# Projection and routing stage: the weights of the chosen experts made on GpSimd instead of VectorE

## The chip, the cores and the metric

One core of one Trainium2 chip runs the whole kernel. The metric is the device time of one execution in microseconds. Times of the trace are counted from the start of the profiled execution's span.

## The reference, cut to what matters

The model has two layers, each with an attention and a mixture of experts. Only the stage behind the first attention is touched: projection, layer norm, residual, layer norm, and the choice of 6 of 64 experts for each of N = 8192 tokens.

```python
x = x + _layernorm(attention(x) @ w_proj)
logits = _layernorm(x) @ router_weight.T
scores = jax.nn.sigmoid(logits)
_, top_idx = jax.lax.top_k(scores + expert_bias[None, :], K)        # E = 64, K = 6
top_scores = jnp.take_along_axis(scores, top_idx, axis=1)
probs = top_scores / (jnp.sum(top_scores, axis=-1, keepdims=True) + 1e-20)
```

## The kernel before

The kernel is a chain of phases with a barrier of all engines between them. The phase in question, `phase_project_route` (tiles prj_...), works on 16 blocks of 512 tokens. A block is four tiles of 128 tokens (TPB = 4), with the tokens on the partitions; j is the block's parity and picks one of two buffers. The program of each engine is written by hand, in order, with semaphores. `pipeline(e, stages, 4)` runs the steps: in step n each engine calls `stages(a, b, c, d)` with a = block n, b = block n-1, c = block n-2 and d = block n-3, so that four blocks are in work at a time. There are 19 steps; a block that isn't there yet or any more is None.

- a: VectorE divides the attention output by its denominators (L988, `att`), ScalarE rounds it to `ah` (L1089), VectorE makes the rest `al` (L1048).
- b: TensorE multiplies by the projection, 24 matmuls into `y_ps`. VectorE takes mean and variance (L745 to L750), GpSimd makes 1/sqrt as a power of -0.5 (L949), VectorE the shift (L756), ScalarE the normalised `yn` (L1095, four instructions), GpSimd the residual sum `xo` (L954).
- c: VectorE takes the statistics of `xo`, GpSimd the power (L945), VectorE the shift (L756), ScalarE writes the normalised rows to `xn[:, j, t, 0:C]` (L1083, four instructions). TensorE turns them, ScalarE and VectorE make the two parts `xh` (L1103) and `xl` (L1052).
- d: TensorE makes the logits (24 matmuls), ScalarE the sigmoid `sc` (L1072). VectorE chooses: `choose` adds the bias, finds the largest with MAX8, copies 6 of them to `pick` beside two fill values (L1009), replaces them (L1012) and writes the 0/1 `mask` (L1014). TensorE packs the mask (L1155). VectorE's `weigh` multiplies the scores by the mask, sums over the experts, adds 1e-20, takes the reciprocal and writes the 64 weights to `xn[:, j, :, C:XW]`, beside the rows of the same tokens (L1023 to L1028). SyncE (SP) stores `xn[:, j]`, rows and weights together, to `expert_rows` (L905).

`xn` has two buffers. ScalarE waits ahead of L1083 until the stores out of `xn[:, j]` that belong to the block two before have landed:

```python
e.wait_ge(r_stored[j], R_STORES)
e.wait_ge(x_scale, 1)
```

SP's queue holds, in each step: load of x, store of xo; stores of xh and xl; loads of the attention output and denominators; store of the packed mask; store of xn. `step` (class Chain) makes an engine wait for its own last instruction before it goes on.

Of the kernel before, what the change touches and what calls it, by code (L numbers as in the profile page):

```python
# [8 lines left out]
ALU = mybir.AluOpType  # L9
ACT = mybir.ActivationFunctionType  # L10
AX = mybir.AxisListType


B, T, C = 8, 1024, 256
N = B * T
NH, HD = 16, 16
P = 128
# [20 lines left out]
def take(eng, *pairs):  # L38

    for sem, n in pairs:  # L40
        eng.sem_inc(sem, -n)  # L41
# [718 lines left out]
def phase_project_route(nc, layer, o_d, rden_d, x_d, wp_d, rw_d, rb_d, yb_d, xo_d, xh_d, xl_d, xg_d, rt_d):  # L760
# [7 lines left out]
    with Phase(nc, f"prj{layer}") as ph:  # L768
# [24 lines left out]
        sb = ph.sb("sb", [P, TPB, E + 8 - K])  # L793
        rep = ph.sb("rep", [P, TPB, E + 8 - K])
        top = ph.sb("top", [P, TPB, 8])
        pick = ph.sb("pick", [P, TPB, 8])
        mask = ph.sb("mask", [P, TPB, E])
        ssum = ph.sb("ssum", [P, TPB])
        rt = ph.sb("rt", [E, 2, BLK // PACK])
# [45 lines left out]
        choice_turned = ph.sem("choice_turned")  # L845
        rt_ready = ph.sem("rt_ready")
        weights_ready = ph.sem("weights_ready")
        xo_seen = ph.sem("xo_seen")
        xo_stored = [ph.sem(f"xo_stored{j}") for j in range(2)]
        x_stored = [ph.sem(f"x_stored{j}") for j in range(2)]  # L850
# [16 lines left out]
        with nc.Block() as block:  # L867
# [61 lines left out]
            @block.gpsimd  # L929
            def _(e):  # L930
                step = Chain(e, pool_chain)
                identity(e, step, ident)
                step(e.memset(digits[:], 0.0))
                for n in range(PACK):
                    step(e.affine_select(out=digits[:], in_=digits[:], compare_op=ALU.not_equal,
                                         fill=float(2 ** (PACK - 1 - n)), base=-n, pattern=[[-PACK, P // PACK]],
                                         channel_multiplier=1))
                step(e.memset(mhalf[:], -0.5))
                e.sem_inc(pe_consts, 1)
                step.close()  # L940

                def stages(a, b, c, d):
                    if c is not None:
                        e.wait_ge(xvar_ready, 1)
                        e.tensor_tensor(rs[:, 1], ve[:, 1], mhalf[:], ALU.pow).then_inc(xrstd_ready, 1)  # L945
                        take(e, (xvar_ready, 1))
                    if b is not None:
                        e.wait_ge(yvar_ready, 1)
                        e.tensor_tensor(rs[:, 0], ve[:, 0], mhalf[:], ALU.pow).then_inc(yrstd_ready, 1)  # L949
                        j = b[1]  # L950
                        e.wait_ge(x_loaded[j], 16)
                        e.wait_ge(xo_stored[j], 16)
                        e.wait_ge(yn_ready, 1)
                        e.tensor_tensor(xo[:, j], x[:, j], yn[:], ALU.add).then_inc(xo_ready, 1)  # L954
                        take(e, (yvar_ready, 1), (x_loaded[j], 16), (xo_stored[j], 16), (yn_ready, 1))

                pipeline(e, stages, 4)

            @block.vector
            def _(e):  # L960
                step = Chain(e, dve_chain)
                e.wait_ge(den_loaded[0], 16)
                e.reciprocal(den[:, 0], den[:, 0]).then_inc(rden_ready[0], 1)
                e.wait_ge(den_loaded[1], 16 * (B - 1))
                e.reciprocal(den[:, 1:B], den[:, 1:B]).then_inc(rden_ready[1], 1)
                e.wait_ge(w_loaded, 48 if layer == 0 else 64)
                split_weights(e, step, wf, wh, wl)
                step(e.memset(sb[:, :, E:E + 8 - K], 3e38))
                step(e.memset(pick[:, :, K:8], 3e38))
                e.sem_inc(pe_consts, 1)  # L970
                step.close()

                def residual(j):
                    e.wait_ge(xo_ready, 1)
                    e.sem_inc(xo_seen, 1)
                    variance(e, step, xo[:, j], st[:, 1], mv[:, 1], ve[:, 1], xvar_ready)
                    take(e, (xo_ready, 1))

                def projected():
                    e.wait_ge(y_ready, 1)  # L980
                    if layer == 1:
                        step(e.tensor_tensor(y[:], y_ps[:], ybias[:].unsqueeze(1).broadcast_to((P, TPB, C)), ALU.add))
                    variance(e, step, y, st[:, 0], mv[:, 0], ve[:, 0], yvar_ready)
                    take(e, (y_ready, 1))

                def divide(j):
                    e.wait_ge(o_loaded[j], 4 * 16)
                    e.tensor_tensor(att[:], o[:, j], rden[:, j], ALU.mult).then_inc(att_ready, 1)  # L988
                    take(e, (o_loaded[j], 4 * 16))

                def softmax_shift():
                    e.wait_ge(logits, 1)
                    step(e.reduce_max(lmax[:], l_ps[:], AX.X))
                    e.tensor_tensor(ls[:], l_ps[:], lmax[:].unsqueeze(2).broadcast_to((P, TPB, E)), ALU.subtract
                                    ).then_inc(shifted, 1)
                    take(e, (logits, 1))

                def choose(j):
                    e.wait_ge(scores, 1)
                    if layer == 1:  # L1000
                        step(e.reduce_sum(ssum[:], sc[:, j], AX.X))
                        step(e.reciprocal(ssum[:], ssum[:]))
                        step(e.tensor_tensor(sc[:, j], sc[:, j], ssum[:].unsqueeze(2).broadcast_to((P, TPB, E)), ALU.mult))
                    step(e.tensor_tensor(sb[:, :, 0:E], sc[:, j], rbias[:].unsqueeze(1).broadcast_to((P, TPB, E)),
                                         ALU.add))
                    for t in range(TPB):
                        e.max(top[:, t], sb[:, t, 0:E])
                    step.settle()
                    step(e.tensor_copy(pick[:, :, 0:K], top[:, :, 0:K]))  # L1009

                    for t in range(TPB):
                        e.match_replace(rep[:, t], pick[:, t], sb[:, t], -3e38)  # L1012
                    step.settle()
                    choice = e.tensor_scalar(mask[:], rep[:, :, 0:E], -1e38, None, ALU.is_lt)  # L1014
                    if layer == 0:
                        choice.then_inc(choice_ready, 1)
                        step.settle()
                    else:
                        step(choice)
                    take(e, (scores, 1))  # L1020

                def weigh(j):
                    step(e.tensor_tensor(sc[:, j], sc[:, j], mask[:], ALU.mult))  # L1023
                    step(e.reduce_sum(ssum[:], sc[:, j], AX.X))
                    step(e.tensor_scalar(ssum[:], ssum[:], 1e-20, None, ALU.add))
                    step(e.reciprocal(ssum[:], ssum[:]))
                    weights = xn[:, j, :, C:XW] if layer == 0 else mask[:]
                    e.tensor_tensor(weights, sc[:, j], ssum[:].unsqueeze(2).broadcast_to((P, TPB, E)), ALU.mult  # L1028
                                    ).then_inc(weights_ready if layer == 0 else choice_ready, 1)

                def stages(a, b, c, d):
                    if c is not None:
                        residual(c[1])
                    if b is not None:
                        projected()
                    if c is not None:
                        scaling(e, mv[:, 1], rs[:, 1], nmr[:, 1], xrstd_ready, x_scale)
                    if a is not None:
                        divide(a[1])
                    if layer == 1 and d is not None:  # L1040
                        softmax_shift()
                    if b is not None:
                        scaling(e, mv[:, 0], rs[:, 0], nmr[:, 0], yrstd_ready, y_scale)
                    if d is not None:
                        choose(d[1])
                    if a is not None:
                        e.wait_ge(ah_ready, 1)
                        e.tensor_tensor(al[:], att[:], ah[:].bitcast(fp32), ALU.subtract).then_inc(al_ready, 1)  # L1048
                        take(e, (ah_ready, 1))
                    if c is not None:  # L1050
                        e.wait_ge(xh_ready, 1)
                        e.tensor_tensor(xl[:, c[1]], t_ps[:], xh[:, c[1]].bitcast(fp32), ALU.subtract  # L1052
                                        ).then_inc(xl_ready, 1)
                        take(e, (xh_ready, 1))
                    if d is not None:
                        weigh(d[1])
                    step.close()

                pipeline(e, stages, 4)
# [1759 lines left out]
```

## Time and profile before

| what | us |
|---|---|
| median of 3 runs | 3260.66 (3260.47 to 3262.6) |
| the profiled execution | 3258.48 |
| its span | 3256.8 |
| VectorE busy over the span | 2225.7 (68%) |
| TensorE matmuls busy | 2842.0 (87%) |
| GpSimd busy | 731.5 (22%) |

The phase lies between about 1080 and 1353 us of the span. Busy shares are sums over the whole kernel; what a change in this phase is worth is read from this phase. A row of the timeline gives start, duration, engine, line, operation, output and inputs, how many instructions it merges, and in brackets the idle time ahead of it with what ended it.

### The profile page before, as it was taken

Reading aid. Unit: us, or ns where it says so; the run is one execution under the profiler, and the core shown is the slowest. Engines: PE = TensorE matmul, PEld = TensorE weight load, DVE = VectorE, ACT = ScalarE, POOL = GpSimd, SP = SyncE. Lnnn points to the kernel's source line nnn. Section 1 sums busy time; section 2 is a strip of 40 time slices with the busy share of each in tenths; the row PEclk is TensorE's granted clock in tenths of the full one; section 3 lists DMA queues with packets and bytes.
Section 4 is the critical chain, followed back from the end, with each engine's and each line's share of the span. In section 5 each row is a group of like instructions: output and inputs, shape, how many; then the busy total and the mean of one; then the engine's idle time right before and its main releaser. Section 6 shows DMA issues by size and latency. Waiting matters only on the chain. (4 is left out here: it accounts for less than half of the span.)

```text
span 3256.8 us, 59136 instructions
## 1 busy us (share of the span) xinstructions
PE 2842.0 (87%) x20033; PEld 2062.9 (63%) x20033; DVE 2225.7 (68%) x6134; ACT 1603.0 (49%) x2446; POOL 731.5 (22%) x882
## 2 busy tenths in 40 slices
PE   7959999999999387689947777998399999999998
PEld 6834444444444276578836664555388888888887
DVE  6768999999997388663338883444466666666664
ACT  3506777777777244333325544544244444444443
POOL 1022222222222133247744422222000000000000
PEclk9959999999999666699968888999699999999999
DMA  6984556666662377648857867653432424243331
GB/s 244 330 153 83 108 115 112 112 112 116 112 110 65 127 270 269 214 138 225 221 165 269 296 228 228 183 162 100 132 99 74 122 65 117 78 102 92 90 86 46
DMA packets 342662, 485.87 MB, mean 149 GB/s; under 512 B 58832, under 2 KB 203248, under 8 KB 342384
## 3 DMA queue, kind: packets, MB, share of 16 engines
q1 hardware_dynamic: 331776, 468.94, 52.1%
q0 software_dynamic: 10240, 14.16, 2.3%
q8 instruction: 85, 1.39, 0.2%
q10 hardware_dynamic: 496, 0.84, 0.1%
q14 instruction: 65, 0.53, 0.1%
HBM read 278.77 MB, written 204.53 MB: 148 GB/s over the span
## 5 line engine op out<-in xcount | busy, mean ns | idle before, releaser
L551 ACT ACTIVATE att_pr<-att_e_ps 128x1024 f32<-128x1024 f32 (+2 forms) x640 | 567.3, 938 | 203.8 <-PE att_e_ps L603 203.8
L579 PE MATMUL att_m_ps<-att_ks,att_qs 63*128 63x512 f32 (+3 forms) x1536 | 465.9, 433 | 40.2 <-PEq L41 31.7
L513 DVE CUSTOM_DVE_ANT_0 att_kept<-att_m_ps,att_causal 128x256 f32<-128x256 f32 (+3 forms) x1024 | 448.5, 488 | 50.3 <-DVEq L41 21.9
L579 PEld LDWEIGHTS att_m_ps<-att_ks,att_qs 63*128 63x128 f32 x1536 | 234.3, 189 | 370.6 <-DVE att_mx L516 148.5
L492 POOL TENSOR_SCALAR_AFFINE_SELECT att_pr<-att_pr 128x256 f32<-128x256 f32 (+1 forms) x384 | 181.4, 485 | 698.0 <-PEq L594 694.5
L516 DVE TENSOR_REDUCE att_mx<-att_m_ps 128x1 f32<-128x512 f32 x512 | 323.3, 684 | 21.5 <-PE att_m_ps L579 17.5
L623 PE MATMUL att_o_ps<-att_pr,att_vs 128*32 128x512 f32 (+3 forms) x3072 | 328.7, 501 | 3.7 <-issue 2.0
L2604 ACT ACTIVATE fin_hh<-fin_hid 128x512 fp32r<-128x512 f32 x192 | 121.4, 632 | 399.8 <-DVE fin_hid L2450 302.2
L603 PE MATMUL att_e_ps<-att_qs,att_ks 64*128 64x512 f32 (+3 forms) x1536 | 269.1, 376 | 6.7 <-ACT att_pr L551 3.3
L2343 POOL TENSOR_TENSOR fin_rs<-fin_ve,fin_mhalf 128x4 f32<-128x4 f32 x48 | 48.4, 1007 | 928.6 <-POOLq L41 928.6
L2446 DVE TENSOR_TENSOR fin_hid<-fin_gate,fin_u_ps 128x512 f32<-128x512 f32 x192 | 131.5, 685 | 136.4 <-ACT fin_gate L2598 82.9
L738 PE MATMUL fin_f_ps<-fin_fhd,fin_hh 128*128 128x256 f32 x768 | 219.5, 286 | 0.2 <-DVE fin_hl L2465 0.2
L738 PE MATMUL fin_f_ps<-fin_fhd,fin_hl 128*128 128x256 f32 x768 | 216.3, 282 | 0.0
L738 PE MATMUL fin_f_ps<-fin_fld,fin_hh 128*128 128x256 f32 x768 | 216.2, 282 | 0.0
L2465 DVE TENSOR_TENSOR fin_hl<-fin_hid,fin_hh 128x512 fp32r<-128x512 f32 x192 | 132.5, 690 | 104.5 <-ACT fin_hh L2604 100.8
L1949 DVE TENSOR_TENSOR lin_am<-lin_a_ps,lin_tri 128x512 f32<-128x512 f32 x128 | 88.5, 692 | 143.5 <-PE lin_a_ps L2032 143.5
L603 PEld LDWEIGHTS att_e_ps<-att_qs,att_ks 64*128 64x128 f32 x1536 | 150.1, 187 | 38.8 <-ACT att_pr L551 13.5
L738 PE MATMUL fin_u_ps<-fin_xh,fin_fhu 128*128 128x512 f32 x384 | 153.0, 398 | 0.0
L738 PE MATMUL fin_g_ps<-fin_xh,fin_fhg 128*128 128x512 f32 x384 | 152.5, 397 | 0.0
L738 PE MATMUL fin_g_ps<-fin_xh,fin_flg 128*128 128x512 f32 x384 | 151.9, 396 | 0.0
L738 PE MATMUL fin_u_ps<-fin_xh,fin_flu 128*128 128x512 f32 x384 | 151.6, 395 | 0.0
L738 PE MATMUL fin_u_ps<-fin_xl,fin_fhu 128*128 128x512 f32 x384 | 151.5, 394 | 0.0
(332 smaller groups left out, 6921.2 us busy)
## 6 DMA issues: line engine op xcount, KB each, us to landing
fin_raw<-weights SPq DMA_DIRECT2D x32, 1024.0 KB, 9.6
att_qs<-q_high SPq DMA_DIRECT2D x128, 128.0 KB, 5.2
att_ks<-k_high SPq DMA_DIRECT2D x128, 128.0 KB, 6.5
attended<-att_ot SPq DMA_DIRECT2D x64, 256.0 KB, 8.5
acc<-att_zero SPq DMA_DIRECT2D x64, 256.0 KB, 2.2
moe_w<-w SPq DMA_DIRECT2D x128, 128.0 KB, 3.4
lqk_a<-acc SPq DMA_DIRECT2D x32, 512.0 KB, 6.0
attended<-lin_ot SPq DMA_DIRECT2D x32, 512.0 KB, 3.7
```

The costliest lines, as they stand in the source:

```text
L492: e.affine_select(out=blk, in_=blk, compare_op=ALU.is_ge, fill=0.0, base=0, pattern=lead + [[1, P]], channel_multiplier=-1).then_inc(maske ...
L513: e.tensor_tensor_reduce(kept[:, n % MBUF, 0:w], m_ps[:, n % MBUF, 0:w], causal[:, BLK - w:], 1.0, -3e38, ALU.add, ALU.max, mx[:, h, at, q ...
L516: e.reduce_max(mx[:, h, at, q:q + 1], m_ps[:, n % MBUF, 0:w], AX.X).then_inc(m_free, 1)
L551: e.activation(out, src, ACT.Exp).then_inc(exp_done, 1)
L579: e.matmul(m_ps[:, (2 * i + n) % MBUF, 0:w], qs[rows, j, p, q * P:(q + 1) * P], ks[rows, j, p, h * BLK:h * BLK + w], start=True, stop=True ...
L603: i = e.matmul(e_ps[:, s % 2, n, m * w:(m + 1) * w], ks[rows, j, p, k * P:(k + 1) * P], qs[rows, j, p, (h + 1) * BLK - w:(h + 1) * BLK], s ...
L623: i = e.matmul(o_ps[32 * hd:32 * hd + 32, BLK - w:BLK], vs[:, j, k, hd * VW:hd * VW + 32], pr[:, u % NPR, hd // 2, hd % 2, 0:w], start=k = ...
L738: i = e.matmul(out, a, b, start=first and n == 0, stop=last and n == len(terms) - 1, **kw)
L1949: e.tensor_tensor(am[:, n % 2, 0:F // 2].rearrange("p (r h) q -> p r h q", h=2), a_ps[:, 0:2, 0:2 * P].rearrange("p r (h q) -> p r h q", h=2),
L2446: product_ = e.tensor_tensor(hid[:, c % 2], gate[:, c % 2], u_ps[:, c % 2], ALU.mult)
L2465: e.tensor_tensor(hl[:, c % 3], hid[:, c % 2], hh[:, c % 3].bitcast(fp32), ALU.subtract).then_inc(hl_ready, 1)
L2604: e.activation(hh[:, c % 3], hid[:, c % 2], ACT.Copy).then_inc(hh_ready, 1)
```

## The change

In `phase_project_route` alone. VectorE's `weigh` goes; GpSimd does the same work for block d behind its residual sum of block b. It multiplies scores by mask, adds the two halves of the 64 values six times (32, 16, 8, 4, 2, 1 values for each token), adds 1e-20, raises to the power -1 and multiplies. Two semaphores are new: VectorE tells GpSimd that the mask is ready (mask_ready), and waits before it writes the next mask until GpSimd has read this one (mask_read). The copy to `pick` goes: MAX8 now reads all 66 columns of `sb`, of which two hold 3e38, so its eight largest are the two fill values and the six chosen, and serve the replacement directly.

```diff
-        pick = ph.sb("pick", [P, TPB, 8])
+        minus1 = ph.sb("minus1", [P, TPB])
+        half = ph.sb("half", [P, TPB, E // 2])
...
+        mask_ready = ph.sem("mask_ready")
+        mask_read = ph.sem("mask_read")
...
+                step(e.memset(minus1[:], -1.0))
...
                         e.tensor_tensor(xo[:, j], x[:, j], yn[:], ALU.add).then_inc(xo_ready, 1)
                         take(e, (yvar_ready, 1), (x_loaded[j], 16), (xo_stored[j], 16), (yn_ready, 1))
+                    if d is not None:
+                        j = d[1]
+                        e.wait_ge(mask_ready, 1)
+                        step(e.tensor_tensor(sc[:, j], sc[:, j], mask[:], ALU.mult))
+                        e.sem_inc(mask_read, 1)
+                        src, n = sc[:, j], E // 2
+                        while n:
+                            step(e.tensor_tensor(half[:, :, 0:n], src[:, :, 0:n], src[:, :, n:2 * n], ALU.add))
+                            src, n = half, n // 2
+                        step(e.tensor_scalar(ssum[:], half[:, :, 0], 1e-20, None, ALU.add))
+                        step(e.tensor_tensor(ssum[:], ssum[:], minus1[:], ALU.pow))
+                        e.tensor_tensor(xn[:, j, :, C:XW], sc[:, j], ssum[:].unsqueeze(2).broadcast_to((P, TPB, E)),
+                                        ALU.mult).then_inc(weights_ready, 1)
+                        take(e, (mask_ready, 1))
+                        step.close()
+
+                e.sem_inc(mask_read, 1)
...
-                step(e.memset(pick[:, :, K:8], 3e38))
...
-                        e.max(top[:, t], sb[:, t, 0:E])
+                        e.max(top[:, t], sb[:, t])
                     step.settle()
-                    step(e.tensor_copy(pick[:, :, 0:K], top[:, :, 0:K]))
                     for t in range(TPB):
-                        e.match_replace(rep[:, t], pick[:, t], sb[:, t], -3e38)
+                        e.match_replace(rep[:, t], top[:, t], sb[:, t], -3e38)
                     step.settle()
-                    choice = e.tensor_scalar(mask[:], rep[:, :, 0:E], -1e38, None, ALU.is_lt)
-                    if layer == 0:
-                        choice.then_inc(choice_ready, 1)
-                        step.settle()
-                    else:
-                        step(choice)
+                    e.wait_ge(mask_read, 1)
+                    e.tensor_scalar(mask[:], rep[:, :, 0:E], -1e38, None, ALU.is_lt).then_inc(choice_ready, 1)
+                    step.settle()
+                    e.sem_inc(mask_ready, 1)
+                    take(e, (mask_read, 1))
                     take(e, (scores, 1))
-
-                def weigh(j):
-                    step(e.tensor_tensor(sc[:, j], sc[:, j], mask[:], ALU.mult))
-                    step(e.reduce_sum(ssum[:], sc[:, j], AX.X))
-                    step(e.tensor_scalar(ssum[:], ssum[:], 1e-20, None, ALU.add))
-                    step(e.reciprocal(ssum[:], ssum[:]))
...
-                    if d is not None:
-                        weigh(d[1])
```

## Rows read from the trace of the kernel before

**Rows 1.** Busy us (instructions) of PE, PEld, DVE, ACT, POOL in one step; clock, DMA.

```profile
1200.89:1214.79 13.90, 11.06 (x66) 9.80 (x66) 11.68 (x43) 6.39 (x13) 4.53 (x3) 0.62 0.83 284
```

**Rows 2.** Timeline of one step.

```profile
1199.77 1.91 ACT L1095 ACTIVATE prj_yn<-prj_y_ps,prj_nmr,prj_rs 128x256 f32<-128x256 f32 x4
...
1200.89 1.23 DVE L1048 TENSOR_TENSOR prj_al<-prj_att,prj_ah 128x1024 fp32r<-128x1024 f32 x1 [0.25 <-DVEq L709]
1201.85 2.51 POOL L954 TENSOR_TENSOR prj_xo<-prj_x,prj_yn 128x1024 f32<-128x1024 f32 x1 [4.14 <-ACT prj_yn L1095]
...
1202.17 0.58 PE L738 MATMUL prj_y_ps<-prj_wh,prj_ah 128*128 128x256 f32 x1 [0.41 <-DVE prj_al L1048]
...
1204.13 0.51 DVE L1023 TENSOR_TENSOR prj_sc<-prj_sc,prj_mask 128x256 f32<-128x256 f32 x1
...
1205.55 0.42 DVE L1028 TENSOR_TENSOR prj_xn<-prj_sc,prj_ssum 128x256 f32<-128x256 f32 x1
...
1206.13 0.40 SPq L905 DMA_DIRECT2D expert_rows<-prj_xn  x1
...
1207.13 0.28 PE L738 MATMUL prj_y_ps<-prj_wh,prj_al 128*128 128x256 f32 x1
...
1208.31 1.43 DVE L745 BATCH_NORM_STATS2 prj_st<-prj_y_ps 128x6 f32<-128x256 f32 x4
...
1210.05 0.38 ACT L1072 ACTIVATE prj_sc<-prj_l_ps 128x256 f32<-128x256 f32 x1 [6.94 <-PE prj_l_ps L738]
...
1210.48 0.16 DVE L756 SCALAR_TENSOR_TENSOR prj_nmr<-prj_mv,prj_rs 128x4 f32<-128x4 f32 x1
...
1210.74 2.08 ACT L1083 ACTIVATE prj_xn<-prj_xo,prj_nmr,prj_rs 128x256 f32<-128x256 f32 x4 [0.31 <-DVE prj_nmr L756]
...
1213.04 0.18 DVE L1009 COPY prj_pick<-prj_top 128x24 f32<-128x24 f32 x1
1213.25 0.09 DVE L1012 MATCH_VALUE_LOAD prj_rep<-prj_pick,prj_sb 128x8 f32 x1
...
1213.68 1.90 ACT L1095 ACTIVATE prj_yn<-prj_y_ps,prj_nmr,prj_rs 128x256 f32<-128x256 f32 x4
...
1214.79 1.22 DVE L1048 TENSOR_TENSOR prj_al<-prj_att,prj_ah 128x1024 fp32r<-128x1024 f32 x1 [0.25 <-DVEq L709]
...
1216.89 1.23 DVE L1052 TENSOR_TENSOR prj_xl<-prj_t_ps,prj_xh 128x1024 fp32r<-128x1024 f32 x1 [0.87 <-ACT prj_xh L1103]
```

**Rows 3.** DMA issues of the phase: count, KB each, median us to landing.

```profile
expert_rows<-prj_xn SPq DMA_DIRECT2D x16, 640.0 KB, 3.5
```

**Rows 4.** Groups of GpSimd: count, busy us, mean ns of one, idle before.

```profile
L1678 POOL TENSOR_TENSOR lqk_a<-lqk_a 128x1024 f32<-128x1024 f32 x16 | 48.7, 3042 | 1.3
L1677 POOL TENSOR_TENSOR lqk_a<-lqk_a 128x1024 f32<-128x1024 f32 x16 | 37.7, 2355 | 99.3 <-DMA lqk_a<-shared 99.3
L1338 POOL TENSOR_TENSOR moe_hl<-moe_hg,moe_hh 128x512 fp32r<-128x512 f32 x24 | 31.0, 1294 | 39.8 <-ACT moe_hg L1459 38.6
L945 POOL TENSOR_TENSOR prj_rs<-prj_ve,prj_mhalf 128x4 f32<-128x4 f32 x16 | 16.3, 1018 | 59.8 <-POOLq L41 59.8
```

**Rows 5.** GpSimd's chained instructions at the phase's start: one group, then timeline.

```profile
L935 POOL TENSOR_SCALAR_AFFINE_SELECT prj_digits<-prj_digits 128x32 f32<-128x32 f32 x4 | 0.9, 214 | 0.6
1080.87 1.28 POOL L935 TENSOR_SCALAR_AFFINE_SELECT prj_digits<-prj_digits 128x32 f32<-128x32 f32 x4
1082.21 0.10 POOL L938 MEMSET prj_mhalf<- 128x4 f32 x1
```

**Rows 6.** Timeline: first and last steps that have weights.

```profile
1145.05 1.91 ACT L1095 ACTIVATE prj_yn<-prj_y_ps,prj_nmr,prj_rs 128x256 f32<-128x256 f32 x4
...
1332.85 2.06 ACT L1083 ACTIVATE prj_xn<-prj_xo,prj_nmr,prj_rs 128x256 f32<-128x256 f32 x4
...
1346.33 0.29 DVE L1014 TENSOR_SCALAR prj_mask<-prj_rep 128x256 f32<-128x256 f32 x1
...
1348.20 0.43 DVE L1028 TENSOR_TENSOR prj_xn<-prj_sc,prj_ssum 128x256 f32<-128x256 f32 x1
```

More of the change, by code:

```diff
@@ L1006, in choose @@
                     for t in range(TPB):
-                        e.max(top[:, t], sb[:, t, 0:E])
+                        e.max(top[:, t], sb[:, t])
                     step.settle()
-                    step(e.tensor_copy(pick[:, :, 0:K], top[:, :, 0:K]))
                     for t in range(TPB):
-                        e.match_replace(rep[:, t], pick[:, t], sb[:, t], -3e38)
+                        e.match_replace(rep[:, t], top[:, t], sb[:, t], -3e38)
                     step.settle()
-                    choice = e.tensor_scalar(mask[:], rep[:, :, 0:E], -1e38, None, ALU.is_lt)
-                    if layer == 0:
-                        choice.then_inc(choice_ready, 1)
-                        step.settle()
-                    else:
-                        step(choice)
-                    take(e, (scores, 1))
-                def weigh(j):
-                    step(e.tensor_tensor(sc[:, j], sc[:, j], mask[:], ALU.mult))
-                    step(e.reduce_sum(ssum[:], sc[:, j], AX.X))
-                    step(e.tensor_scalar(ssum[:], ssum[:], 1e-20, None, ALU.add))
-                    step(e.reciprocal(ssum[:], ssum[:]))
-                    weights = xn[:, j, :, C:XW] if layer == 0 else mask[:]
-                    e.tensor_tensor(weights, sc[:, j], ssum[:].unsqueeze(2).broadcast_to((P, TPB, E)), ALU.mult
-                                    ).then_inc(weights_ready if layer == 0 else choice_ready, 1)
+                    e.wait_ge(mask_read, 1)
[3 more added lines that the diff above has]
+                    take(e, (mask_read, 1))
+                    take(e, (scores, 1))
                 def stages(a, b, c, d):
```

## The prediction

> **What bounds the kernel now.** I read the stage's totals first. One step of the pipeline (one block of 512 tokens) lasts 13.9 us here, with VectorE busy 11.68 and TensorE 11.06 us, ScalarE 6.39 and GpSimd 4.53 us [rows 1]. VectorE's busy time leaves out the gaps of its chained instructions, so the second view is one step on the timeline [rows 2]. The subtraction at L1048 starts at 1200.89 and again at 1214.79: 13.90 us. In between VectorE waits once for work of another engine, 0.87 us before L1052, for ScalarE; the rest is its own instructions and their gaps. So VectorE sets the step, and `weigh` takes 1204.13 to 1205.97 of it, 1.84 us, some 2.0 with the gap ahead of the next statistics.
>
> Then I looked for what comes next if VectorE gets shorter. TensorE's product y runs from 1202.17 to 1207.41 (5.24 us), and its statistics start only at 1208.31: 0.9 us of slack. GpSimd's addition (L954) starts 0.17 us behind the end of ScalarE's L1095 (1199.77 + 1.91 = 1201.68) and takes 2.51 us. ScalarE runs L1083, L1089 and L1095 without a hole from 1210.74 to 1215.58, 4.84 us. And ahead of L1083 it waits on the semaphore r_stored[j]: the stores of the row buffer xn[:, j], the same buffer that `weigh` filled one step earlier, must have landed. That store is issued at 1206.13, 0.16 us behind the weights, and takes 3.5 us to land [rows 3]: 1209.6, against L1083's start at 1210.74. This wait is hidden with 1.1 us to spare. I take it as the important number of this trace.
>
> **The change part by part.** *Removed from VectorE:* five instructions of `weigh`, 2.0 us a step; the copy to `pick`, 0.18 us and its gap, 0.21 in all (L1009 starts at 1213.04, L1012 at 1213.25) [rows 2]. MAX8 reads 66 instead of 64 columns, the memset goes: nothing that counts. If nothing else were late, the step would fall only until y bounds it: L1048's end to y's start 0.05, y 5.24, handover some 0.08, and from y's statistics (1208.31) to L1048's end (1216.01) 7.70 less the copy's 0.21; 12.9 us. So the gain is at most 1.0 of the 2.2 us.
>
> *Added to VectorE:* a wait for mask_read ahead of the mask. GpSimd gives it behind its first multiplication, a good part of a step earlier, so nothing. Choosing now always settles, which the first layer did before too.
>
> *Added to GpSimd*, in order behind L954 of the same step: a 128x256 multiplication, six additions of 128, 64, 32, 16, 8 and 4 elements a partition, an addition of a constant to 4, a power of 4, and a 128x256 multiplication; each waits for the one before. No small addition stands in the trace, so I fit one. 128x512 takes 1.29 us and 128x1024 2.355 us (L1338, L1677) [rows 4]: 2.07 ns an element and 0.23 us fixed. So a multiplication of 256 takes 0.76; the six additions hold 252 elements, 6 x 0.23 + 252 x 0.00207 = 1.90; the constant about 0.2 (between the 0.10 of a memset [rows 5] and the 0.24 of the fit); the power 1.02 (L945, the same shape). Together 4.64 us. The gap between chained instructions: four selects of 214 ns each in 1.28 us, that is (1.28 - 0.21)/3 - 0.21 = 0.14 us [rows 5]; nine gaps, 1.3 us, and 0.1 to start. I call the whole W: 6.0 us. Lower bound: small instructions at the memset's 0.10 + elements (1.1 instead of 1.90, constant 0.1), gaps the same: 5.0. Upper bound: multiplications slowed as L1678's mean is (3.04 for 2.36) [rows 4], additions on strided views at 0.4 each, gaps of 0.2: 7.8. I take the fit, since the sizes lie between its own points and the 4-element power.
>
> *Moved:* the weights' end. It was 1205.97, or 1.6 us behind L954's end; it becomes W behind it. Queued behind it: on GpSimd the two powers of the next step (which VectorE's L756 needs), on SP the store of the rows, and behind that store everything SP issues for the next step (the load of x, the stores of x, x_high, x_low, the loads of o). Those transfers are wanted a step or more later, and their buffers are free; they cost nothing. The row store is what counts. In the new order, with T the end of L1095:
> - L954 starts at T + 0.17 and ends at T + 2.68; weights at T + 2.68 + W; the store is issued 0.16 later and lands 3.5 later: T + 6.34 + W. Only then may ScalarE start L1083 of the next step, and T comes again 4.84 later.
> - The step is 0.17 + 2.51 + W + 0.16 + 3.5 + 4.84 = 11.18 + W = 17.2 us for 13.90.
> - The other way through GpSimd is shorter: power 1.02, handover 0.1, L756 0.16, handover 0.1 behind the weights, instead of 3.66.
> - L1083 also stands behind L1072, which needs the logits. y starts 0.49 us behind T (1202.17 against 1201.68) and took 5.24 us for 24 matmuls, most of it at the lower clock (0.62 granted over the step [rows 1], where 0.5 would be 1.2 GHz throughout). If the 24 matmuls of the logits took as long, as an estimate, L1072 (0.38 us) would end at T + 0.49 + 5.24 + 5.24 + 0.4 = T + 11.4, still before T + 12.3. This becomes the floor (a step of 16.2 us) only for W below 5.0.
>
> A rule that bears on W: the Trainium skill, "GPSIMD Engine Reference", Performance versus the Vector engine, holds a two-input elementwise instruction to be about half as fast on GpSimd as on VectorE, 4497 ns for 2048 elements; my fit gives 0.23 + 4.24 = 4.47 us for that size, so the trace agrees on the slope. The same rule carried to this whole chain is the second rival below.
>
> **Sum over the phase** [rows 6]. The weights of the first block are made in the step whose L1095 ends at 1146.96. The next L1083 comes at 1146.96 + 0.17 + 2.51 + W + 0.16 + 3.5 = 1153.30 + W. Thirteen more steps follow to the last L1083 (was 1332.85); the last but one has no L1089 (the 0.86 us between L1083's end at 1212.82 and L1095's start, and what it overlaps; I take 1.0) [rows 2]: 1153.30 + W + 13 x (11.18 + W) - 1.0 = 1297.6 + 14 W. Behind it the last block's chain runs as before, to the mask (ends 1346.62), and then the weights come W + 0.1 later, not 2.0 us (L1028 ends 1348.62), less 0.2 for the copy; nothing hides this, as ScalarE waits for that store before the phase ends. The difference is 14 W - 35.2 + W - 2.1 = 15 W - 37.3. For W = 6.0: +52.7 us. Against the profiled execution's own 3258.5 us this gives 3311; the median of the runs is 2.2 us above it, so 3313. W's bounds give 15 x 5.0 - 37.3 = +37.7 (3298) and 15 x 7.8 - 37.3 = +79.7 (3340). The change loses nothing only if W is below 2.5 us.
>
> **The rivals.**
> - *GpSimd's chain is cheap, and the kernel gets faster.* Place: the ten instructions behind L954. It decides if W is under 2.5 us. Each microsecond below that gives 15; at W = 1.7 the 12.9 us that y allows take over, and the change is worth 15 x 1.7 - 37.3 = -12: 3249. Against it: one power and two multiplications alone are 2.5 [rows 4]. Chance 0.02.
> - *GpSimd takes twice what VectorE took.* The five instructions took VectorE 1.84 us with their gaps, some 1.7 without; twice that, with four gaps of 0.14 between them, is 3.4 to 3.9 us. At W = 3.9 the sum gives +21; if the floor of the logits holds instead, the steps are those of W = 5.0, +37 less 1 at the end: 3282 to 3297. That is the rule of the Trainium skill named above, taken as a whole (its Key points: structurally about twice as fast on VectorE). Against it: the fixed 0.23 us counts ten times here, and a 4-element power takes 1.02 where VectorE's reciprocal takes 0.18. Chance 0.10.
> - *The store isn't what is waited for* (it lands sooner, or its wait is over in time). Then the power bounds: 0.17 + 2.51 + W + 1.02 + 0.36 + 4.84 = 8.9 + W = 14.9 us a step, 2.3 less than forecast in 14 steps: +52.7 - 32 = +21, 3281. At W = 5.0 about +6 remains, which is within what can be told. For it: no row shows ScalarE waiting for this store now. Against it: the code's wait and the measured landing. Chance 0.06, 0.03 of it within 0.2%.
> - *W above 7.0*, strided small additions or VectorE's use of the shared memory slowing GpSimd: 3330 and more. Chance 0.15.
> - My forecast, W from 4.9 to 7.0 with the store as the wait: 0.67, with a range of its own of 3296 to 3328.
>
> **The numbers.** 3313 us. 0.2% (6.5 us) is about what a measurement of this kernel can tell from no change. Faster 0.02, same 0.03, slower 0.95. The range takes in the lower bound of W, part of the second rival, and the upper bound: 3288 to 3338.
>
> **What the profile of the changed kernel would show.** Steps of about 17.2 us in this phase and nothing changed elsewhere; GpSimd with ten more instructions a step over 5 to 7 us, small additions near 0.25 us and gaps near 0.15; L905's counterpart issued about 8.8 us behind L1095's end, landing in 3.3 to 3.8; ScalarE's L1083 idle until then, with the row store or SP as its releaser; VectorE with long waits where it had one of 0.87; TensorE's granted clock no better than now (0.62). The prediction is wrong if small additions take 0.1 us or 0.5 us, if L1083 starts before the store has landed, or if the row store, now alone and early in its queue, lands in much under 3.3 us.

## The result: slower, by 25 to 28 us and in a second set of runs by 35 to 38

| kernel | median us | ratio to before (95%) | profiled execution | the stage in it |
|---|---|---|---|---|
| before | 3260.47 (5 runs) | | 3258.48 | 274.9 |
| changed | 3285.6 (5 runs) | 1.0085 (1.0069 to 1.0101) | 3287.37 | 310.1 |
| changed, timed again (4 runs, against 7 of before) | 3294.93 | 1.0115 (1.0094 to 1.0136) | 3295.24 | 309.0 |

The medians differ by 25.1 us in the first set and by 34.9 in the second; the ratios stand for 27.7 and 37.5 us, and their intervals overlap.

"The stage" is the time from GpSimd's first instruction on prj_ident to its first on moe_ident, the identity matrices that each phase makes at its start; it is the finest measure in what follows, since the rest of the kernel differs by several us from one execution to the next. It comes from one profiled execution of each kernel; the two of the changed kernel differ by 1.1 us, most of it before the first normalised rows, so a difference of about 1 us between stages says nothing by itself. The step lengths agree much better.

Four rows of the waits in the changed kernel, 1130 to 1375 us (who waited for whom, us in total, times, longest):

```profile
ACT prj_xn L1089 <- DMA expert_rows<-prj_xn: 39.9, 14, 3.6
DVE prj_xl L1060 <- ACT prj_xh L1109: 32.5, 16, 3.7
DVE prj_al L1056 <- ACT prj_ah L1095: 21.6, 12, 1.8
DVE prj_nmr L756 <- POOL prj_rs L949: 16.7, 14, 3.7
```

The first line is new: fourteen times, once a step, ScalarE stands ahead of the normalised rows until the store of rows and weights has landed. VectorE, which waited only 0.87 us in a step [rows 2], now waits for ScalarE and for GpSimd's power.

One step's busy times (us and instructions of PE, PEld, DVE, ACT, POOL; granted clock, DMA), beside [rows 1]:

```profile
1200.69:1216.76 16.07, 11.63 (x64) 10.47 (x64) 9.93 (x38) 6.39 (x13) 8.54 (x13) 0.61 0.73 242
```

VectorE has 1.75 us less to do and GpSimd 4.0 more, TensorE is the busiest with 72%, and the step is 2.2 us longer: no engine's work fills it, so the bound is a chain of waits. One step on the timeline, ScalarE, GpSimd and SP (L1101, L1089, L958, L949 and L908 here are L1095, L1083, L954, L945 and L905 of before):

```profile
1203.61 1.90 ACT L1101 ACTIVATE prj_yn<-prj_y_ps,prj_nmr,prj_rs 128x256 f32<-128x256 f32 x4
...
1214.20 0.38 ACT L1078 ACTIVATE prj_sc<-prj_l_ps 128x256 f32<-128x256 f32 x1 [7.25 <-PE prj_l_ps L738]
1216.76 2.08 ACT L1089 ACTIVATE prj_xn<-prj_xo,prj_nmr,prj_rs 128x256 f32<-128x256 f32 x4 [2.17 <-DMA expert_rows<-prj_xn]
...
1219.68 1.90 ACT L1101 ACTIVATE prj_yn<-prj_y_ps,prj_nmr,prj_rs 128x256 f32<-128x256 f32 x4
```

```profile
1205.69 2.38 POOL L958 TENSOR_TENSOR prj_xo<-prj_x,prj_yn 128x1024 f32<-128x1024 f32 x1 [6.73 <-ACT prj_yn L1101]
1208.02 0.73 POOL L963 TENSOR_TENSOR prj_sc<-prj_sc,prj_mask 128x256 f32<-128x256 f32 x1
1208.93 0.45 POOL L967 TENSOR_TENSOR prj_half<-prj_sc 128x128 f32<-128x128 f32 x1 [0.18 <-POOL prj_sc L963]
1209.46 1.51 POOL L967 TENSOR_TENSOR prj_half<-prj_half 128x64 f32<-128x64 f32 x5
1211.07 0.23 POOL L969 TENSOR_SCALAR prj_ssum<-prj_half 128x4 f32<-128x4 f32 x1
1211.38 1.04 POOL L970 TENSOR_TENSOR prj_ssum<-prj_ssum,prj_minus 128x4 f32<-128x4 f32 x1
1212.49 0.61 POOL L971 TENSOR_TENSOR prj_xn<-prj_sc,prj_ssum 128x256 f32<-128x256 f32 x1
1213.06 1.01 POOL L949 TENSOR_TENSOR prj_rs<-prj_ve,prj_mhalf 128x4 f32<-128x4 f32 x1
```

```profile
1213.27 0.40 SPq L908 DMA_DIRECT2D expert_rows<-prj_xn  x1
```

This is the loop of the prediction, link by link: L1101 ends at 1205.51; 0.18 later GpSimd's addition, 2.38; the chain to 1213.10, W = 5.03; 0.17 to the store's issue; 3.49 until L1089 starts; 4.82 until L1101 ends again at 1221.58. The sum is 16.07 us, for 13.64 and 13.9 by turns before (13.77 on the mean). The last block adds its own: its mask is written at 1372.98 and its weights at 1378.29, 5.3 us later where it was 2.0.

### The profile page after: what moved, and what is told of

The parts are those of the page before. It is cut to its first block and busy times, and to the rows that moved or that the text cites. A ratio compares the mean times of both kernels' runs of the same rounds, so it can differ in the third digit from the quotient of the medians.

```text
span 3285.6 us, 59297 instructions
## 1 busy us (share of the span) xinstructions
PE 2843.0 (87%) x20033; PEld 2068.9 (63%) x20033; DVE 2200.1 (67%) x6037; ACT 1602.9 (49%) x2446; POOL 797.7 (24%) x1043
## 5 line engine op out<-in xcount | busy, mean ns | idle before, releaser
L738 PE MATMUL fin_g_ps<-fin_xl,fin_fhg 128*128 128x512 f32 x384 | 151.5, 395 | 0.0
```

The source lines that it names most:

```text
L738: i = e.matmul(out, a, b, start=first and n == 0, stop=last and n == len(terms) - 1, **kw)
```

## The experiments

The stage of each profiled execution, and the whole kernel's ratio to the kernel before (3 or 5 rounds each, 4 to 12 runs):

| run | stage us | against 274.9 | ratio (95%) |
|---|---|---|---|
| e1_copy_only | 274.4 | -0.5 | 1.0011 (0.9994 to 1.0027) |
| e2_weigh_early | 280.2 | +5.3 | 1.0023 (1.0009 to 1.0037) |
| e3_own_store | 285.1 | +10.2 | 1.0037 (1.0022 to 1.0051) |
| e4_one_more_power | 326.7 | +51.8 | 1.0160 (1.0131 to 1.0189) |
| e5_step_later | 278.7 | +3.8 | 0.9996 (0.9980 to 1.0012) |
| e6_weigh_early_two_inputs | 279.1 | +4.2 | 1.0021 (1.0006 to 1.0036) |
| e7_rows_early | 284.8 | +9.9 | 1.0027 (1.0015 to 1.0039) |
| e8_step_later_rows_early | 278.7 | +3.8 | 1.0011 (0.9996 to 1.0026) |
| e9_no_store_waited | 277.4 | +2.5 | 1.0018 (1.0002 to 1.0034) |
| e10_weigh_sums_in_psum | 273.5 | -1.4 | 0.9998 (0.9986 to 1.0011) |
| e11_score_between_rows | 268.3 | -6.6 | 0.9987 (0.9971 to 1.0003) |
| e12_changed_again | 309.0 | +34.1 | 1.0115 (1.0094 to 1.0136) |

### What is the chain's length worth: e4

```diff
                         step(e.tensor_tensor(ssum[:], ssum[:], minus1[:], ALU.pow))
+                        step(e.tensor_tensor(half[:, :, 0], half[:, :, 1], minus1[:], ALU.pow))
```

> The changed kernel with one more power of 4 elements in GpSimd's chain, its result unused; W goes from 5.1 to 6.2 us. My theory: the whole chain lies on the loop, so each microsecond of W costs 15: 16.5 us above the changed kernel, step 17.2 us. Rival (part of the chain is still covered by something else that is as late): under 8 us.

The stage went from 310.1 to 326.7, 16.6 us for one more power of 1.04 us and its gap, with steps of 17.19 us on the median. Against the changed kernel's other profiled execution (309.0) it is 17.7. Every microsecond of the chain costs 15 to 16, as the sum said; nothing else covers any of it.

### Is it the store that is waited for: e3, e7, e9

```diff
+        wts = ph.sb("wts", [P, 2, TPB, E])
...
-                            e.wait_ge(weights_ready, 1)
-                            e.dma_start(tiles(xg_d[0:N])[d[0], d[1]], xn[:, d[1]]).then_inc(r_stored[d[1]], 16)
+                            e.dma_start(rows[:, :, 0:C], xn[:, d[1], :, 0:C]).then_inc(r_stored[d[1]], 16)
+                            e.wait_ge(weights_ready, 1)
+                            e.dma_start(rows[:, :, C:XW], wts[:, d[1]]).then_inc(w_stored[d[1]], 16)
```

> The changed kernel, but the weights have a buffer and a store of their own, so that ScalarE's wait ahead of the normalised rows is only for the store of the rows, which no longer waits for GpSimd. GpSimd does the same instructions at the same place. My theory (the store behind GpSimd's chain is what is waited for): the step falls from 16.1 us to the one through GpSimd's power, 8.9 + 5.1 - 0.1 = 13.9 us, and the kernel to within 0.2% of the one before, 2 to 6 us above it for the last block. Rival (GpSimd's own time in the loop costs it all): the step stays at 16.1 and the kernel 28 us above the one before.

The stage fell by 25.0 of the 35.2 us, with GpSimd's instructions and their order unchanged. But about half of the steps took 13.7 us and the others up to 15.5. ScalarE still waited 10.0 us in seven steps:

```profile
ACT prj_xn L1097 <- DMA expert_rows<-prj_xn: 10.0, 7, 2.3
```

SP issued this store behind its loads and the packed mask, and it landed 6.2 us after its issue (median), where the joint store of more bytes took 3.5, before as after the change; why is not shown. So it was moved up:

```diff
                         e.dma_start(turned(xl_d)[d[0], j], xl[:, j].bitcast(fp32)).then_inc(x_stored[j], 16)
+                        e.dma_start(tiles(xg_d[0:N])[d[0], j][:, :, 0:C], xn[:, j, :, 0:C]).then_inc(r_stored[j], 16)
```

> The changed kernel with a buffer and a store of its own for the weights, and the store of the rows now issued right behind the stores of xh and xl, some 8 us earlier in SP's queue than in the run before, where ScalarE still waited for it 10 us in all. My theory: that wait goes, every step is 13.7 to 13.9 us (GpSimd's power), and the stage takes 278 to 280 us against 275 before: 3 to 5 us slower than before. Rival: the moved store makes another transfer late (xh, xl or the loads) and the stage stays at 285.

The expectation fell and the rival held: the stage stayed at 284.8. The waits show why (1150 to 1330 us):

```profile
ACT prj_xn L1097 <- DMA chosen<-prj_rt: 8.6, 8, 1.8
```

r_stored counts two stores, and now the other one, the packed mask of 32 KB behind a megabyte of loads, came last: 6.0 us from issue to landing on the median, for 3.6 in e3. So the moved store had made another transfer late, though not one that the rival named. e9 gave the packed mask's store a semaphore of its own, waited for ahead of the instruction that writes the packed mask:

```diff
+                        e.wait_ge(rt_stored[d[1]], 16)
                         e.activation(rt[:, d[1]], r_ps[:], ACT.Copy).then_inc(rt_ready, 1)
```

> The changed kernel with an own buffer and store for the weights, the rows stored early, and the semaphore of the packed mask's store taken out of ScalarE's wait ahead of L1083: it is now waited for only ahead of the instruction that writes the packed mask. GpSimd's work and order are those of the changed kernel. My theory: in the runs before, the steps in which no store was waited for took 13.7 us, the others up to 15.8; now all take 13.7 to 13.9, and the stage 277 to 279 us, 3 to 4 above the kernel before for the last block (chain of 5.1 instead of 2.0 us). Rival: GpSimd's chain ahead of the power has a cost of its own, steps above 14.3 and a stage above 283.

Steps of 13.84 to 13.86 us with one of 14.1, a stage of 277.4: another 7.4 us are gone, and 2.5 remain. Between the first and the last normalised rows it takes 1.9 us more than before, some 0.08 a step; behind them, with the last block, another 1.9; and the start took 1.3 less, as it can by chance (e12's took 1.0 less). So with no store on the loop, GpSimd's five microseconds cost next to nothing a step. VectorE's two free ones gain nothing either (1150 to 1330 us):

```profile
DVE prj_nmr L756 <- POOL prj_rs L954: 15.4, 13, 3.7
ACT prj_xn L1099 <- DVE prj_nmr L756: 7.5, 11, 1.1
```

VectorE, 2 us shorter, waits 1.2 us a step for the power that stands behind GpSimd's chain, and ScalarE for VectorE: the 8.9 + W = 13.9 us of the prediction's third rival.

### Can GpSimd's idle time hide the chain: e5, e8

GpSimd makes the weights one step later, ahead of its residual sum, with a buffer and a store of their own; e8 also stores the rows early.

```diff
+                    if g is not None:
+                        weigh(g[1])
+                    if b is not None:
                         j = b[1]
                         e.wait_ge(x_loaded[j], 16)
```

> The changed kernel with the weights in a buffer and store of their own and made on GpSimd one step later, between its power for the projection's statistics and its residual sum, where it idled about 4 us before. My theory: the chain no longer stands ahead of the power that VectorE waits for; the residual sum starts about 1 us later than ScalarE's L1095 would allow. The step is 13.0 to 13.5 us, the stage 2 to 8 us shorter than with the kernel before's 275, less about 3 for the last block and less what ScalarE waits for the rows' store (10 us in all in the run with an own store). In sum 272 to 282. Rival: GpSimd's chain again sets the step, since the residual sum now follows it, and the step stays above 13.9.

> As the one with the weights a step later, and the rows stored right behind xh and xl. My theory: with no store waited for, the step is 13.0 to 13.5 us and the stage 268 to 275 us against 275 before: 0 to 7 us faster. Rival: the chain ahead of the residual sum sets the step at 13.9 or above, and the stage is no shorter than before.

Both stages took 278.7 us, most steps 13.8 to 14.0; in both the rival was right. In e5 ScalarE already waited for no store, so the early one of e8 had nothing to gain. Rows of e5 show the loop, GpSimd and then VectorE:

```profile
1209.11 0.88 POOL L955 TENSOR_TENSOR prj_prod<-prj_sc,prj_mask 128x256 f32<-128x256 f32 x1
...
1215.13 2.39 POOL L985 TENSOR_TENSOR prj_xo<-prj_x,prj_yn 128x1024 f32<-128x1024 f32 x1 [0.51 <-POOLq L41]
...
1222.11 1.01 POOL L977 TENSOR_TENSOR prj_rs<-prj_ve,prj_mhalf 128x4 f32<-128x4 f32 x1 [1.16 <-DVE prj_ve L750]
```

```profile
1217.66 1.40 DVE L745 BATCH_NORM_STATS2 prj_st<-prj_xo 128x6 f32<-128x256 f32 x4 [2.02 <-POOL prj_xo L985]
...
1219.81 1.43 DVE L745 BATCH_NORM_STATS2 prj_st<-prj_y_ps 128x6 f32<-128x256 f32 x4
```

The chain starts behind the power for y, and that power needs y's statistics, which VectorE makes behind those of the residual sum. So the chain (6.0 with the gap behind it), the sum 2.4, both sets of statistics 4.6 and the power 1.0 stand in one loop: 13.97. The two expectations had left this loop out.

### What was VectorE's time worth: e1, e2, e6, e10, e11

e1 takes out the copy alone, as the changed kernel does.

> The kernel before with only the copy to pick taken out (MAX8 over all 66 columns); the weights stay on VectorE. My theory: the loop that sets the step of 13.9 us goes through ScalarE (its rounding of xh ends only 0.87 us after VectorE has stopped to wait), then VectorE's xl, weigh and statistics. The copy lies beside ScalarE's part, so VectorE only waits 0.2 us longer there: 0 us gained, at most 1. Rival: VectorE's own time sets the step, then 0.21 us in each of 14 steps: 3 us faster.

Steps of 13.54 and 13.81 by turns, 0.1 less than before; the wait for xh grew from 0.87 to 1.08 in the step shown (0.92 to 1.12 on the mean of 13), so the copy's 0.21 went mostly into it. The stage is 0.5 us shorter, which by itself is within chance. e2 also fills that wait:

```diff
+                    if d is not None:
+                        weigh(d[1])
                     if c is not None:
                         e.wait_ge(xh_ready, 1)
...
-                    if d is not None:
-                        weigh(d[1])
                     step.close()
```

> The kernel before without the copy, and with VectorE's weigh called one place earlier, behind al and ahead of xl, where VectorE now waits 0.87 us for ScalarE. My theory: the wait is filled, VectorE's instructions then need 12.8 us a step and TensorE's product with its statistics 12.9, so the step falls from 13.9 to 12.9 us: 12 us faster over the stage (3248 against 3260). Rival: xl, 1.1 us later behind al, makes the logits or a transfer late, and the step stays within 0.3 us of 13.9: 0 to 4 us.

It was slower, and for a reason that I hadn't thought of. VectorE's and GpSimd's rows of one step:

```profile
1202.07 0.42 DVE L1020 TENSOR_TENSOR prj_sc<-prj_sc,prj_mask 128x256 f32<-128x256 f32 x1
1202.52 0.42 DVE L1021 TENSOR_REDUCE prj_ssum<-prj_sc 128x4 f32<-128x256 f32 x1
1202.97 1.77 DVE L1022 TENSOR_SCALAR prj_ssum<-prj_ssum 128x4 f32<-128x4 f32 x1
1204.78 0.18 DVE L1023 RECIPROCAL prj_ssum<-prj_ssum 128x4 f32<-128x4 f32 x1
```

```profile
1202.08 2.63 POOL L953 TENSOR_TENSOR prj_xo<-prj_x,prj_yn 128x1024 f32<-128x1024 f32 x1 [4.14 <-ACT prj_yn L1092]
```

An addition of a constant to 4 elements takes 1.77 us, here and on the median of its 16, instead of the 0.17 of before. It ends at 1204.74, GpSimd's addition at 1204.71. e6 replaced it by an instruction with two SBUF tiles, e10 kept it and put `ssum` into PSUM:

```diff
-                    step(e.tensor_scalar(ssum[:], ssum[:], 1e-20, None, ALU.add))
+                    step(e.tensor_tensor(ssum[:], ssum[:], tiny[:], ALU.add))
```

```diff
-        ssum = ph.sb("ssum", [P, TPB])
+        ssum = ph.ps("ssum", [P, TPB])
```

> The kernel with weigh ahead of xl again, but the constant 1e-20 is added by an instruction with two input tiles (tensor_tensor) instead of one input and a constant. In the run before it that tensor_scalar on 4 elements a partition took 1.77 us (median of 16) instead of 0.17, and ended when GpSimd's 128x1024 addition ended. My theory: only this form of VectorE's instruction waits for GpSimd's running one; with two input tiles it takes 0.2, the step falls from 13.98 to about 12.9 us and the stage gets 10 to 13 us shorter than before's 275. Rival: VectorE is held whatever the form, or the reciprocal behind it takes over the wait: the step stays at 13.9 to 14.0.

> The kernel before without the copy, weigh on VectorE ahead of xl, and the tile of the sums (ssum, 4 elements a partition) in PSUM instead of SBUF, so that the constant's addition has no SBUF operand and the last multiplication only one. My theory: the instruction of 4 elements took 1.77 us in both runs with weigh early because VectorE needed for it the SBUF interface that GpSimd's addition of 128x1024 held; with operands in PSUM it takes 0.2 us, nothing is held up, the step falls from 13.98 to 12.9 to 13.1 us, and the stage is 8 to 13 us shorter than the kernel before's 275. Rival: it is the order that holds VectorE (an instruction behind a reduction, or GpSimd running at all); it takes 1.7 us again and the step stays at 13.98.

With two SBUF tiles it took 1.76 us on the median, again to the end of GpSimd's instruction (1203.39 against 1203.36), so my theory of the form fell:

```profile
1201.62 1.77 DVE L1024 TENSOR_TENSOR prj_ssum<-prj_ssum,prj_tiny 128x4 f32<-128x4 f32 x1
1200.72 2.64 POOL L954 TENSOR_TENSOR prj_xo<-prj_x,prj_yn 128x1024 f32<-128x1024 f32 x1 [4.14 <-ACT prj_yn L1094]
```

With the tile in PSUM, at the same place, it takes what it took before:

```profile
L1022 DVE TENSOR_SCALAR prj_ssum<-prj_ssum x16: 170/170/171, 1144.6 to 1343.4; 128x4 f32<-128x4 f32 x16
```

So it is the SBUF operands of these two forms, and not the order; the reduction ahead of them (L1021) has SBUF operands too and kept its 0.42 us. The Trainium skill, "SBUF — State Buffer", SBUF: two separate sides, says that VectorE and GpSimd share one pair of ports as an exclusive lock: a GpSimd instruction and a VectorE instruction in a two-port mode, or one with two SBUF inputs where GpSimd reads SBUF, block each other, and whichever starts first keeps the pair to its end. Both slow forms (1.77 and 1.76 us) and the fast one (0.17) agree with it. But e10's step is 13.65, not the 12.9 of my estimate, and the stage only 1.4 us shorter than before. Its waits (1150 to 1330 us):

```profile
PE prj_y_ps L738 <- ACTq L1095: 11.4, 12, 1.0
DVE prj_st L745 <- PE prj_y_ps L738: 9.3, 12, 0.8
```

TensorE's product waits for ScalarE to let go of y_ps. ScalarE was late because it makes the scores, which wait for TensorE's logits, ahead of the rows, whose shift VectorE had ready at 1205.92:

```profile
1205.76 0.16 DVE L756 SCALAR_TENSOR_TENSOR prj_nmr<-prj_mv,prj_rs 128x4 f32<-128x4 f32 x1
1206.44 0.38 ACT L1069 ACTIVATE prj_sc<-prj_l_ps 128x256 f32<-128x256 f32 x1 [7.10 <-PE prj_l_ps L738]
1206.72 2.06 ACT L1080 ACTIVATE prj_xn<-prj_xo,prj_nmr,prj_rs 128x256 f32<-128x256 f32 x4
```

e11 moves the scores:

```diff
                             e.activation(xn[:, j, t, 0:C], xo[:, j, t], ACT.Identity, bias=nmr[:, 1, t:t + 1],
                                          scale=rs[:, 1, t:t + 1]).then_inc(xn_ready, 1)
+                            if t == 1 and d is not None:
+                                score(d[1])
```

> The run before (VectorE's weigh ahead of xl, sums in PSUM, no copy) with one more edit: ScalarE makes the scores of block d (which wait for TensorE's logits) between the second and third of the four normalised tiles of block c instead of ahead of them. In that run the step was 13.65 us, with ScalarE waiting for the logits ahead of its rows, and TensorE's next product starting when ScalarE had let go of y_ps. My theory: once VectorE has 2 us to spare, the loop is TensorE's product and logits (8.0 us), then the scores and ScalarE's rows, ah and yn (5.1 us): taking the scores out of the way shortens it by 0.3 to 0.5 us, a step of 13.2 to 13.35 us and a stage of 268 to 271 us against 273.5. Rival: the later scores hold up VectorE's choice and al by as much as ScalarE gains, the step stays at 13.6 or rises.

L1045 starts at 1199.16, 1212.53 and 1225.20: steps of 13.4 and 12.7, 13.1 on the mean of twelve, and a stage of 268.3, 6.6 us shorter than before. So the order was what held e10. The whole kernel's ratio, 0.9987 (0.9971 to 1.0003), fits that and can't be told from no change.

### The changed kernel once more: e12

> The changed kernel, unaltered, profiled and timed once more. Its first profile had the stage 35.2 us longer than the kernel before's, but the attention stage 6.4 us shorter (889.6 against 896.0), and the times differed by 28. My theory: the attention stage differs from execution to execution and has nothing to do with the change; in this profile it takes 890 to 896 at random, the stage again 310 us, and the median over more runs lies 28 to 37 us above the kernel before's. Rival: the changed program always has the shorter attention stage (889 to 890), and the difference stays at 25 to 28.

The attention stage took 896.3 us here and 889.6 in the first profile, with the same instructions; over all profiled executions, of before and of the experiments, it lies between 889.6 and 896.3. The routing stage took 309.0 and 310.1. So the first profile's total (+28.9 us) is its stage (+35.2) with 6.4 us of that chance taken off. That the same holds for the unprofiled runs of the first set was not shown, since they have no trace; the second set gave 1.0115, which is +37 us.

## Why the prediction was right, and where it was off

- *The store behind GpSimd's chain becomes what is waited for*: right, in place and in mechanism. L1089 waits for it in 14 steps; e3, e7 and e9 took the two stores out of the loop one by one and got back 32.7 of 35.2 us. The rival "the store isn't what is waited for" is out, but its own number was right: with the store away the step is 13.85 us, by GpSimd's power.
- *The sum 11.18 + W*: the fixed part measured 11.04 (L958 took 2.38, not 2.51, now that it starts behind VectorE's al instead of beside it; in e9, where it starts beside it again, it took 2.52).
- *W = 6.0* was mis-sized; it measured 5.03. The last multiplication took 0.61 for 0.76; the six additions 455, 320, 251, 221, 202 and 204 ns, 1.65 in all for 1.90; the nine gaps 0.07 to 0.18, 0.8 in all for 1.3; and nothing passed ahead of the chain, for 0.1. The first multiplication (0.73), the constant (0.23) and the power (1.04) were as estimated. That my lower bound, 5.0, meets the total is luck: it has the additions at 1.1 and the gaps at 1.3, and the two errors cancel. (The upper bound's own terms add up to some 7.5, not 7.8.) In the formula W = 5.03 gives 15 x 5.03 - 37.3 = +38, and the shorter L958 takes 1.7 off: 36.5, where the stages gave 35.2 and 34.1.
- *3313 us*: high by 18 to 27 us, some 14.5 of it from W and 1.7 from L958, and in the first set of runs some 6 more from the attention stage's chance, if it was there too. Of the two medians 3285.6 lies 2 us below the range of 3288 to 3338, 3294.9 inside it.
- *Twice VectorE's time* (W = 3.9): the chain took 5.03 for VectorE's 1.84 us, 2.7 times. The factor of two that the Trainium skill gives in "GPSIMD Engine Reference", Key points, is more than the two multiplications of 256 elements cost (0.73 and 0.61 for VectorE's 0.51 and 0.42, a factor of 1.4) and far less than the sum does: six additions, 1.65 us without gaps, for one reduction of 0.42.
- *At most 1.0 us a step to be gained from VectorE, by y's bound of 12.9*: this step failed. The next bound was not y's length but ScalarE's order, which put TensorE's logits ahead of the rows: 13.65, 0.1 below before. The prediction did have this loop, but at 16.2 us, since it took 5.24 us for the logits. [rows 2] already spoke against that: L1072 ended at 1210.43, 8.75 us behind L1095's end, and with the 4.84 of ScalarE's run that is 13.6, next to e10's 13.65. The same error stands in the second rival, whose floor of 16.2 was none. The loop holds none of VectorE's work on the weights, so by it the change could gain some 0.1 us a step even if GpSimd's part cost nothing; no run made that case. Even with the scores moved (e11) the steps took 13.1 on the mean.
- *Nothing for mask_read*: right in effect. VectorE stood 0.20 us more ahead of the mask, under its other waits.
- *Granted clock no better* (0.61 for 0.62), *steps near 17.2* (16.07), *issue 8.8 behind L1095's end* (7.8), *landing 3.3 to 3.8* (3.1 to 3.6, median 3.5): as the profile was to show, less the 1 us of W.

## What to carry to other kernels

Before work is moved to an engine with idle time, follow what its result releases to the end, transfers included: here a store of 3.5 us with 1.1 us to spare stood behind five instructions that looked like plain VectorE time, and every microsecond of delay cost fifteen. A buffer that holds both an early and a late result ties the early one's release to the late one; two stores under one semaphore do the same. And an engine that looks like the bound by its busy time is worth only the distance to the next loop, which one run with its work filled into a wait can measure.

## Not expected of the hardware

- A VectorE instruction of 4 elements with its operands in SBUF took 1.77 us (one input and a constant) or 1.76 us (two inputs), medians of 16, when it was issued while GpSimd's 128x1024 addition ran, and ended within 0.03 us of it; with operands in PSUM 0.17. A reduction of 256 elements beside the same addition kept its 0.42 us. GpSimd's addition took 2.63 beside them, 2.51 in the kernel before and 2.38 in e10.
- The same at small scale in e5: VectorE's L756 took 0.68 instead of 0.15 us beside GpSimd's multiplication of 0.88.
- Chained GpSimd instructions of 4 to 16 elements took 202 to 221 ns with gaps of 0.08 us, a power of 4 elements 1037 ns.
- The attention stage, the same code each time, took 889.6 to 896.3 us over the fourteen profiled executions.
